# Two graph layers over 64 pairs of graphs: the loop over the pairs written out with constants

## The reference

```python
h = max(layernorm(x), 0)
# first layer: attention weights, then three powers of the transition matrix
Xw = h @ Wv + bv;  sj = Xw @ aw[:d];  si = Xw @ aw[d:]
alpha = A * exp(leaky_relu(sj[None, :] + si[:, None] + ab, 0.2))
T = alpha / (row_sums(alpha) + 1e-12)
H = h @ Wk[0] + (T @ h) @ Wk[1] + (T @ T @ h) @ Wk[2] + biases
x = x + relu(H)
# second layer: three graph convolutions
h = max(layernorm(x), 0)
for W, b in (W1, b1), (W2, b2), (W3, b3):
    h = A @ (h @ W) + b          # relu behind the first two
x = x + h
```

## Time and profile before

| what | us |
|---|---|
| median of 3 runs | 897.61 (896.24 to 898.79) |
| the profiled execution | 896.19 |
| its span, first to last instruction | 894.2 |
| PE busy | 873.0 (98%) |
| DVE busy | 780.2 (87%) |
| ACT busy | 629.5 (70%) |
| POOL busy | 443.3 (50%) |
| TensorE clock granted | 0.994 of full speed |

### The profile page before, as it was taken

The page is one execution under the profiler, slowest core; times in us unless marked ns, Lnnn a source line. Parts: engine busy times, 40 slices in busy tenths (PEclk is TensorE's granted clock), DMA queues, the critical chain, the costliest instruction groups (busy, mean ns, idle before and its releaser), DMA issues.

```text
span 894.2 us, 22245 instructions
## 1 busy us (share of the span) xinstructions
PE 873.0 (98%) x6480; PEld 818.2 (92%) x6480; DVE 780.2 (87%) x2065; ACT 629.5 (70%) x1543; POOL 443.3 (50%) x532
## 2 busy tenths in 40 slices
PE   8799999999999999999999999999999999999996
PEld 7699999899998999989999999998999999999996
DVE  5789999899898999989999899989999899999972
ACT  4477777677777777777777677776777677777773
POOL 4455454455454455455454455454555454555552
PEclk9899999999999999999999999999999999999999
DMA  8112122122121122121121121121121121221001
GB/s 195 41 32 56 35 60 59 32 59 54 34 59 48 41 59 55 34 59 46 43 59 50 39 59 46 43 59 41 48 59 45 44 59 41 48 59 47 26 26 35
DMA packets 107819, 45.44 MB, mean 51 GB/s; under 512 B 72560, under 2 KB 107504, under 8 KB 107760
## 3 DMA queue, kind: packets, MB, share of 16 engines
q1 hardware_dynamic: 106672, 43.81, 19.4%
q10 hardware_dynamic: 1088, 1.05, 0.4%
HBM read 28.05 MB, written 16.78 MB: 50 GB/s over the span
## 4 chain that ended last, share of the span: by engine, by line
PE 92%; issue 2%; DVE 1%; SPq 1%; POOL 1%; ACT 1%; DMA 1%; DVEq 0%; ACTq 0%; POOLq 0%
PE bank L873 41%; PE bank_p L873 35%; PE bank_turned L873 6%; PE bank_T L873 4%; PE bank_turned L884 3%; PE bank_T L894 2%; SPq L272 1%; DMA bias_col<-in_L_gnn_b 1%; ACT s_hi L517 0%; DVE h0T_lo L639 0%; POOL w_gcn_lo L372 0%; DVE p0b L716 0%; PE bank_p L1029 0%; POOL y__lo L345 0%; POOL bias_h L388 0%
## 5 line engine op out<-in xcount | busy, mean ns | idle before, releaser
L345 POOL TENSOR_TENSOR y__lo<-y_full,y__hi 128x256 fp32r<-128x256 f32 x256 | 191.5, 762 | 101.0 <-ACT y_full L534 101.0
L336 POOL TENSOR_TENSOR rstd<-veps,minus_half 128x2 f32<-128x2 f32 x128 | 95.5, 746 | 250.6 <-DVE veps L606 250.6
L873 PE MATMUL bank_p<-w_p_hi,h0T_hi 128*128 128x258 f32 (+1 forms) x512 | 176.4, 360 | 1.0 <-POOL w_p_lo L367 1.0
L873 PE MATMUL bank_p<-w_p_lo,h0T_hi 128*128 128x258 f32 (+1 forms) x512 | 165.3, 339 | 0.0
L873 PE MATMUL bank_p<-w_p_hi,h0T_lo 128*128 128x258 f32 (+1 forms) x512 | 142.7, 340 | 5.9 <-DVE h0T_lo L639 5.9
L873 PE MATMUL bank<-w_gcn_hi,y__hi 128*128 128x256 f32 x512 | 132.9, 292 | 1.5 <-ACT y__hi L534 1.3
L873 PE MATMUL bank<-w_gcn_lo,y__hi 128*128 128x256 f32 x512 | 127.9, 283 | 0.0
L534 ACT ACTIVATE y__hi<-bank,bias_col 128x256 fp32r<-128x256 f32 x256 | 119.8, 468 | 3.0 <-PE bank L873 3.0
L534 ACT ACTIVATE y_full<-bank,bias_col 128x256 f32<-128x256 f32 x256 | 121.7, 475 | 0.0
L361 POOL TENSOR_TENSOR adjT_lo<-adjT_full,adjT_hi 128x256 fp32r<-128x256 f32 x64 | 64.5, 1008 | 85.5 <-ACT adjT_hi L440 85.5
L873 PEld LDWEIGHTS bank_p<-w_p_hi,h0T_hi 128*128 128x128 f32 x512 | 97.3, 190 | 7.2 <-POOL w_p_lo L367 1.2
(11 more groups left out here) (94 smaller groups left out, 2346.7 us busy)
## 6 DMA issues: line engine op xcount, KB each, us to landing
x_in<-in_x SPq DMA_DIRECT2D x64, 256.0 KB, 2.9
x_new<-x_out SPq DMA_DIRECT2D x64, 256.0 KB, 2.2
adj_blocks<-in_adj SPq DMA_DIRECT2D x256, 32.0 KB, 2.1
w_raw<-in_L_gnn_Wk ACTq DMA_DIRECT2D x3, 256.0 KB, 6.9
w_raw<-in_L_gnn_W SPq DMA_DIRECT2D x3, 256.0 KB, 5.8
bk_bc<-in_L_gnn_bk SPq DMA_DIRECT2D x1, 384.0 KB, 6.2
wv_raw<-in_L_gnn_Wv ACTq DMA_DIRECT2D x1, 256.0 KB, 3.7
aw_bc<-in_L_gnn_aw SPq DMA_DIRECT2D x1, 256.0 KB, 5.4
```

The costliest lines, as they stand in the source:

```text
L336: pool.tensor_tensor(rstd[n][k % 2][:], veps[n][k % 2][:], minus_half[:], ALU.pow)\
L345: pool.tensor_tensor(y[n][1][:, c], y_full[n][:, c], plain(y[n][0][:, c]), ALU.subtract)\
L873: return pe.matmul(dst, stationary, moving, start=start, stop=stop, skip_group_check=True)
```

## The change

The loop goes. rounds calls one(i, i % 4) for all 67 rounds with i a constant, on every engine. With this every wait compares with a constant and every address is a constant; the helpers lose the case of a register. Order, buffers and the work of each round stay as they are. The program grows from 4 + 8 + 7 = 19 written rounds to 67.

```diff
--- before.py
+++ after.py
@@ -38,7 +38,6 @@
 
 BUSY_BEFORE, BUSY_BETWEEN, BUSY_SECOND, BUSY_TAIL = 19, 18, 19, 16
 ROUND = 4
-BODY = 2 * ROUND
 LAG_B, LAG_C, LAG_D = 1, 2, 3
 LN_EPS = 1e-5
 DIV_EPS = 1e-12
@@ -214,37 +213,28 @@
         y_lo = [sem(f"y_lo{n}") for n in range(2)]
         out_made = sem("out_made")
 
-        def rounds(eng, one):
-
-
-            for i in range(ROUND):
-                one(i, i)
-            with eng.Fori(0, N_PAIRS // BODY - 1) as turn:
-                for k in range(BODY):
-                    one(turn * BODY + (ROUND + k), k % ROUND)
-            for i in range(N_PAIRS - ROUND, N_PAIRS + LAG_D):
+        def rounds(one):
+
+            for i in range(N_PAIRS + LAG_D):
                 one(i, i % ROUND)
 
         def here(i, lag):
 
-            if isinstance(i, int) and not 0 <= i - lag < N_PAIRS:
-                return None
-            return i - lag
+            return i - lag if 0 <= i - lag < N_PAIRS else None
 
         def first(i):
-            return isinstance(i, int) and i == 0
+            return i == 0
 
         def second(i):
-            return isinstance(i, int) and i == 1
+            return i == 1
 
         def tail(i):
 
-
-            return isinstance(i, int) and i >= N_PAIRS
+            return i >= N_PAIRS
 
         def after(i, n):
 
-            return not isinstance(i, int) or i >= n
+            return i >= n
 
         def landed(i, k):
 
@@ -311,7 +301,7 @@
                 if (n := here(i, LAG_D)) is not None:
                     store(n, (k - LAG_D) % ROUND)
 
-            rounds(sp, one)
+            rounds(one)
             for k in range(ROUND):
                 sp.wait_ge(stored[k], 16 * (N_PAIRS // ROUND))
 
@@ -407,7 +397,7 @@
                 if first(i):
                     gcn_weights_low()
 
-            rounds(pool, one)
+            rounds(one)
 
 
         @block.scalar
@@ -572,7 +562,7 @@
                     y1_high(a, k)
                     adjT_high(a, k)
 
-            rounds(act, one)
+            rounds(one)
 
 
 
@@ -860,7 +850,7 @@
                     y1_low(a, k)
                     p0_bias(a, k)
 
-            rounds(dve, one)
+            rounds(one)
 
 
         @block.tensor
@@ -1071,7 +1061,7 @@
                 if b is not None and not tail(i):
                     z1_product(b)
 
-            rounds(pe, one)
+            rounds(one)
 
 
 _OUT = "x_new"
```

## The result

The median of the written-out kernel is 889.60 us (4 runs, 889.17 to 891.19), against 897.22 before (4 runs, 896.24 to 898.79; the table above has three of them): ratio 0.9917, 95% interval 0.9897 to 0.9936. The profiled execution took 889.90 us with a span of 888.1; before it was 896.19 and 894.2. So the profiled pair shows 6.3 us, the medians 7.6; the difference between the two is within the scatter of the kernel before.

The account below looks back on a forecast made before the run. PE was taken as the bound (92% of the chain, 98% busy), with DVE tied to it each round. 896.19 - 6.8 + 1.2 gave 890.6 us for a profiled execution, 892.0 for the median, range 888.0 to 896.0.

Parts of the forecast that it names:

- The jump: Where loop turns meet, DVE idles ahead of h0T_lo and PE waits; six jumps at 1.16 us go, 7.0 us won.
- The rounds' form: 56 loop rounds take the slower written-out form, POOL's y_low starting later: 13.31 against 13.26 us, 1.7 to 2.8 us lost.
- Late alphas: Once per turn alpha on DVE starts 0.40 us late, costing PE 0.24 us; seven of them gone, 1.7 us won.
- new exposures: Block changes in the longer straight code stall an engine visibly; five taken, 1.2 us lost in all.
- the check: Cross-check of the loop part's gain by terms: jumps, late alphas and the rounds' form give -5.9 to -7.0 us.
- the 6.8: Gain over the loop part: 56 written-out rounds at 13.31, 745.4 us, against the measured 752.2 us.
- The packets: Instruction queue traffic of the longer program, scaled from 19 to 67 rounds: 56 packets on q14 and 46 on q8.
- A: Rival: more is won, the slower form of round does not come back, rounds at 13.26, 888.0 us; chance 0.11.
- B: Rival: little is won, part of DVE's wait at the jump returns at block changes, 895.3 us; chance 0.13.
- C: Rival: slower, code delivery decides through block changes on the DVE and PE chain, 902.0 us; chance 0.06.

Follow-up runs that it names:

- a body that fits: Loop kept on all engines, its body cut from 8 rounds to 4, against the kernel before the change; median 887.89 us, ratio 0.9893.
- the memsets: Four tiny memsets added to DVE's first round, against the written-out kernel with POOL's two waits exchanged: 886.76 us; with two memsets 886.94 us.

## Why the prediction was right

*The jump, -7.0 us.* Right in size, and its cause is now shown and not only read. By the rounds' lengths, the six rounds with a jump were 1.14 to 1.29 us longer than the first round of the first turn, 7.1 us together. With DVE alone written out the loop part falls by 7.67 us (the jumps' 7.0 and what the late alphas lost), with all but DVE written out it rises by 2.25, and with a body that fits, fourteen turns cost 1.1 us together. One reading was wrong in part: of the two packets near each jump only the first lands within DVE's idle time. It starts 1.0 to 1.1 us behind the jump, h0T_lo starts 1.5 to 1.6 us after it has landed, and the second packet starts only then (173.94 against 173.54 at the first jump).

*The rounds' form, +1.7 to +2.8.* Right: 13.31 per round throughout, x1 on DVE at 1.117 us in the median, y_low on POOL 2.10 us after the round's start (105.90 against a start at 103.80). Taken back by the order of waits it is worth 2.05 us. The timeline of POOL and DVE in that round:

```profile
105.90 1.45 POOL L335 TENSOR_TENSOR y__lo<-y_full,y__hi 128x256 fp32r<-128x256 f32 x2 [0.83 <-ACT y_full L524]
```

```profile
106.77 1.12 DVE L726 SCALAR_TENSOR_TENSOR x<-hb,x_in 128x512 f32<-128x512 f32 x1
```

*Late alphas, 1.7 us off, and new exposures, 1.2 us on.* The sum came out near, and its factors did not. The late alphas had cost 1.4 us and not 1.7 (rounds of 13.47 to 13.50 against 13.27). A term was missing from the check: the first round of every turn was 13.35, 0.08 longer, 0.6 us for seven. It did no harm, because the 6.8 was taken from the measured 752.2, which has it. For the exposures I took five at 0.24; there are seven longer rounds (8, 15, 24, 31, 40, 47 and 56) at 13.42 to 13.45, 0.11 to 0.14 above the plain ones, about 0.85 us together. All seven belong to DVE, four at x_out and three at alpha. (POOL has a late place of its own: in round 23 its y_low is 0.3 us late in the three kernels in which it is written out with the old order of waits; the round stays at 13.30.) An exposed block change costs PE half of what it did, because in the written-out form DVE has more time in hand: in a plain round it sits idle 0.11 us ahead of aT_lo, against 0.02 in the loop. DVE's stall itself is of the old size: alpha starts 0.35 to 0.38 us later than in the plain rounds, and in the loop it was 0.35 to 0.37.

```profile
217.27 0.33 DVE L619 TENSOR_SCALAR nshift<-mv,rstd 128x1 f32<-128x1 f32 x2 [0.24 <-POOL rstd L326]
217.89 0.42 DVE L659 SCALAR_TENSOR_TENSOR alpha<-adjT_full,e 128x256 f32<-128x256 f32 x1 [0.29 <-issue]
```

Two arguments of the prediction about these places fail. No multiple of a round, it said, fits a block, so the positions drift; in fact 16 rounds are 7 blocks of 128, and the same places come back. And 106.46 us for the first turn is not 8 rounds of 13.31 but 13.35, six of 13.27 and one of 13.50.

*The packets.* 56 and 46 were forecast for q14 and q8, 57 and 53 are there. PE's 40 new ones cost nothing that a round shows.

*The sum.* Forecast for a profiled execution 890.6, measured 889.9: 56 rounds at 13.31 and 1.2 us against 746.06 measured is 0.5 us too much, and 0.2 us came outside the span. The median fell by 7.6 in place of 5.6; 1.3 of the two us lie between the profiled pair and the medians. Later runs of the kernel before have medians of 896.87 (17 runs) and 896.67 (7), by which the gain is 7.3 and 7.1: so 0.3 to 0.5 of the 1.3 is scatter of the first four runs. To the rest I can put no cause.

*The rivals.* A (rounds at 13.26) did not come by itself, but it was there to be had: 13.27 in every plain round after an exchange of two waits, 887.6 us, and 886.8 with the memsets, where A said 888.0. B and C needed 19 exposures or 17 full ones; there were seven small ones.

What stays open: what DVE does in the 1.5 to 1.6 us between the landing of the first packet behind a jump and h0T_lo, and from what length on a body no longer fits.

## What to carry to other kernels

Before a loop is written out, look at where its turns meet: idle time with no releaser there, on one engine, and instruction packets that recur in every turn say that this engine's body is too long, and half the body does as much as no loop at all (887.9 us against 889.6). Of two waits on one instruction, let the one that ends last be the instruction's own. When every round is the same but some, count the instructions of the engine between them: a few more of no use can move a stall under cover.

## What the runs showed of the hardware that I had not expected

- An engine's loop can jump for nearly nothing as long as its body is short enough: DVE with 242 instructions, ACT with 331 and PE with 1693 jumped without a packet of code; DVE with 476 and PE with 5913 did not (all counted between two jumps in the traces). For ACT this is seen where DVE alone is written out: q14 has 21 packets from 170 to 800 us, one in 30 us, which is what DVE's own straight code needs at 128 instructions a packet. The jump that must fetch costs DVE 1.8 us and PE 2.6 us of idle time.
- DVE's stalls in straight code recur every 16 rounds: 56 instructions a round times 16 is 7 times 128, and the first late record is at the same place modulo 128 in the count of DVE's records (447, 831, 1343), waits of the sequencer included. Each takes 0.35 us of the sequencer, and most have cover: in rounds 5 to 59 of the written-out kernel there are 24 such places, 14 of them with a record that is late by that much, and PE pays for seven.
- On POOL 0.06 us in the start of one subtraction changes a DVE instruction that runs beside it by 0.04 us (1.117 against 1.074 in the median), and PE pays that in every round.
